# A language-model tower in one kernel: elementwise work of the router and the embedding moved from VectorE to GpSimd, with new instruction orders and later or earlier loads

## The reference

```python
# token stage
x = emb[tokens] * sqrt(128) + positional_encoding
q, k, v = x @ Wq + bq, x @ Wk + bk, x @ Wv + bv
scores = einsum('d,bijd->bij', attn_scale, tanh(q[:, :, None, :] + k[:, None, :, :]))
x = layer_norm(x + softmax(scores) @ v @ Wo + bo)
h = layer_norm(x + relu(x @ W1 + bf1) @ W2 + bf2)
# causal attention with 8 heads of width 128
h = h + attention(layernorm(h))
# mixture of experts, 64 experts, the best 2 per token
t = layernorm(h); hr = _ln(t)
probs = softmax(hr @ Wr @ codebook.T / 0.7)
w = top2(probs) / sum(top2(probs))
hmoe = sum_k w_k * expert_k(hr) + 0.25 * shared(hr)
out = h + t + hmoe + ffn(_ln(hmoe))
```

## Time and profile before

| | us |
|---|---|
| median of 3 runs | 885.13 |
| lowest and highest | 883.92, 888.87 |
| the profiled execution: time | 880.4 |
| the profiled execution: span from the first to the last instruction | 878.6 |

### The profile page before, as it was taken

The page is one execution under the profiler, slowest core; times in us unless marked ns, Lnnn a source line. Parts: engine busy times, 40 slices in busy tenths (PEclk is TensorE's granted clock), DMA queues, the critical chain, the costliest instruction groups (busy, mean ns, idle before and its releaser), DMA issues. The chain is left out here.

```text
span 878.6 us, 22649 instructions
## 1 busy us (share of the span) xinstructions
PE 781.5 (89%) x7286; PEld 603.4 (69%) x7286; DVE 656.6 (75%) x2161; ACT 657.5 (75%) x1502; POOL 323.0 (37%) x397
## 2 busy tenths in 40 slices
PE   1777998988998989989899999898889999999798
PEld 0454675665665766756667666665679999999687
DVE  3999889989999999999999999453523435443675
ACT  2787989989898898988998999675335655655454
POOL 3110322325334343353343432444414545545121
PEclk9999999999999999999999999997989999999799
DMA  7239889889889889989898898894199999994411
GB/s 149 65 83 210 190 188 210 194 189 212 186 196 210 187 198 207 197 189 206 181 211 181 182 209 178 195 208 97 45 321 397 377 395 403 307 362 161 150 30 37
DMA packets 82305, 177.77 MB, mean 202 GB/s; under 512 B 8244, under 2 KB 35339, under 8 KB 82240
## 3 DMA queue, kind: packets, MB, share of 16 engines
q1 hardware_dynamic: 65536, 164.01, 74.8%
q0 software_dynamic: 5760, 7.92, 2.7%
q10 hardware_dynamic: 10944, 5.02, 2.1%
HBM read 65.93 MB, written 113.34 MB: 204 GB/s over the span
## 5 line engine op out<-in xcount | busy, mean ns | idle before, releaser
L890 DVE TENSOR_TENSOR arena<-qT,b_qk 128x2304 f32<-128x2304 f32 x128 | 323.8, 2543 | 1.6 <-DVE v_bias L915 0.3
L616 ACT ACTIVATE arena<-arena 128x2304 f32<-128x2304 f32 x128 | 271.6, 2123 | 35.7 <-DVE arena L890 34.4
L1322 PE MATMUL b_s<-arena,apad 128*32 128x192 f32 x3072 | 159.2, 343 | 27.1 <-ACT p L625 18.5
L771 ACT ACTIVATE act_h<-big,arena 128x128 f32<-128x128 f32 x336 | 95.8, 368 | 74.6 <-PE big L1642 70.2
L1322 PEld LDWEIGHTS b_s<-arena,apad 128*32 128x32 f32 x3072 | 89.9, 113 | 83.9 <-issue 41.5
L542 POOL TENSOR_TENSOR kept<-kept,rs 96x384 f32<-96x384 f32 x64 | 52.6, 823 | 208.2 <-DVE rs L1025 208.0
L590 POOL DMA_INDIRECT eo_dram<-gT,toff x84 | 82.5, 982 | 97.2 <-issue 67.1
L668 ACT ACTIVATE kept<-kept,mx 96x96 f32<-96x96 f32 x256 | 92.3, 365 | 13.3 <-DVE mx L1018 13.3
L1642 PE MATMUL big<-hbT,arena 128*128 128x128 f32 x672 | 91.1, 279 | 2.4 <-DVE hbT L1205 1.4
L1642 PEld LDWEIGHTS big<-hbT,arena 128*128 128x128 f32 x672 | 83.4, 195 | 3.2 <-issue 2.3
L1205 DVE TENSOR_SCALAR hbT<-b_t,cols 128x128 f32<-128x128 f32 x84 | 34.4, 409 | 65.4 <-PE b_t L1635 65.4
(11 more groups left out here) (208 smaller groups left out, 1413.8 us busy)
## 6 DMA issues: line engine op xcount, KB each, us to landing
rows_dram<-act_h SPq DMA_DIRECT2D x32, 3096.0 KB
arena<-in_wpack SPq DMA_DIRECT2D x84, 578.0 KB
prT<-rows_dram ACTq DMA_DIRECT2D x76, 64.5 KB
arena<-eo_dram SPq DMA_DIRECT2D x4, 512.0 KB, 7.2
x_dram<-res SPq DMA_DIRECT2D x16, 96.0 KB
out<-of SPq DMA_DIRECT2D x12, 128.0 KB, 1.8
eo_dram<-gT,toff POOLq DMA_INDIRECT x84
rows_dram<-rows_now,slot_now POOLq DMA_INDIRECT x64
```

The source lines that it names most:

```text
L616: act.activation(v, v, ACT.Tanh).then_inc(s["tanh"], 1)
L771: last = act.activation(act_h[:, i, c * TILE:(c + 1) * TILE], big[i][:, c * TILE:(c + 1) * TILE], ACT.Silu, bias=wslot[:, slot, 2 * DFF + ...
L890: dve.tensor_tensor(ring[c % TRING].rearrange("p (x m n) -> p x m n", m=CQ, n=N), qv.unsqueeze(3).to_broadcast([D, SPLIT * QG, CQ, N]), kv ...
L1322: last = pe.matmul(b_s[32 * a:32 * a + 32, 0:SPLIT * N], apad[:, 31 - line:63 - line], t[:, :, a, m, :], start=(line == 0), stop=(line == ...
```

## The change

- `x_rows` moves from DVE to POOL and becomes two instructions there, a multiplication and an addition with a semaphore (`xm`) between them. It stands in front of `keep_x`.
- `both_hot` and `counted` move from DVE to POOL. The second running count leaves `ranks` on DVE and becomes `cumulated` on POOL. DVE keeps `chosen`, `one_hot` and the rest of `ranks`. Semaphores `topf`, `oh1`, `ohs`, `cum` replace links of DVE's own chain.
- The order of POOL's body changes: `root` for x1 stands ahead of `keep_rows`, not behind it.
- The order of PE's body changes: `pr_turn` 0 ahead of `tn_turn`, `router` ahead of `pr_turn` 1, `score` 2 ahead of `attend1`, `attend2` 1 ahead of `heads_v` 3, `score` 3 ahead of `heads_g` 0, `attend2` 2 ahead of `xs_turn`, `attend2` 3 ahead of `ffn1` 0.
- In ACT's body `v_copy` stands ahead of `tanh` 5.
- SP issues the seven loads of `ld_b` only when the gathers of pair 0 have landed.
- `ROWS_FIRST` is 1: one weight is loaded ahead of the first tile rows.
- The exponential of the gaps is computed on POOL, as a power of a constant, in the expert loop behind the store of tile 12, and the weights by DVE in tiles 21 to 23. ACT's exponential and its two table loads in the tail are gone. Two of the last four `shared_rows` move into the first `mixture`, and PE waits for them only in front of its first `last2`.

```diff
-ROWS_FIRST = 3
+ROWS_FIRST = 1
...
+            sp.wait_ge(s["emb0"], 16 * G)
             load(wvT[:, :], io["tok_WvT"], s["ld_b"])
...
-            sp.wait_ge(s["emb0"], 16 * G)
...
+            def x_rows(p):
+                early = known(p) and p < EARLY
+                if early:
+                    pool.wait_ge(s[f"emb{p}"], 16 * G)
+                else:
+                    gate(pool, s["emb2"], 16 * G * (p - (EARLY - 1)))
...
+                pool.tensor_scalar(xs[:, :, :], pair_of(res, p) if early else emb[:, :, :],
+                                   float(np.float32(D) ** np.float32(0.5)), None, ALU.mult).then_inc(s["xm"], 1)
+                pool.wait_ge(s["xm"], p + 1)
+                pool.tensor_tensor(xs[:, :, :], xs[:, :, :], pe_rows[:, :].unsqueeze(1).to_broadcast([N, G, D]),
+                                   ALU.add).then_inc(s["xs"], 1)
+            def both_hot(p):
+                pool.wait_ge(s["oh1"], p + 1)
+                wait(pool, s["cum"], p)
+                pool.tensor_tensor(ohs[:, :, :], oh[:, :, 0, :], oh[:, :, 1, :], ALU.add).then_inc(s["ohs"], 1)
+            def counted(p):
+                pool.wait_ge(s["ohs"], p + 1)
+                pool.tensor_tensor(cums[:, 1, :], cums[:, 0, :], ohs[:, 0, :], ALU.add).then_inc(s["oh"], 1)
+            def cumulated(p):
+                pool.wait_ge(s["rank_ps"], p + 1)
+                pool.tensor_tensor(cums[:, 0, :], cums[:, 1, :], ohs[:, 1, :], ALU.add).then_inc(s["cum"], 1)
...
                 at(n, 5, scatter_rows, 1)
+                at(n, -1, x_rows)
+                at(n, -1, keep_x)
+                at(n, 1, root, "x1")
+                at(n, 4, both_hot)
+                at(n, 4, counted)
                 at(n, 4, keep_rows)
-                at(n, 1, root, "x1")
+                at(n, 4, cumulated)
                 at(n, 2, normalise, 0)
-                at(n, -1, keep_x)
+                at(n, 3, roots_h1)
...
+            def weigh():
+                pool.wait_ge(s["gaps_t"], 1)
+                pool.tensor_tensor(gap_e[:, :], base_e[:, :], gaps_t[:, :], ALU.pow).then_inc(s["gap_e"], 1)
...
+                at(n, 0, v_copy)
                 at(n, 0, tanh, 5)
-                at(n, 0, v_copy)
...
-            act.preload_act_table(ACT.Exp)
-            act.activation(gap_e[:, :], gaps_t[:, :], ACT.Exp, scale=1.0 / TEMP).then_inc(s["gap_e"], 1)
-            act.preload_act_table(ACT.Silu)
...
+                at(n, 3, pr_turn, 0)
                 at(n, 4, tn_turn)
...
+                at(n, 0, score, 2)
                 at(n, 1, attend1)
-                at(n, 0, score, 2)
```

More of the change, by code:

```diff
@@ L62 @@
 MASKED = 1.0e30
-DVE_LINKS = 14
+DVE_LINKS = 11
 WCOLS = 2 * DFF + FC + D
@@ L879, in qk_evac @@
             def qk_evac(p):
+                if known(p) and p == 0:
+                    dve.wait_ge(s["consts"], 1)
                 dve.wait_ge(s["qk"], p + 1)
@@ L1223, in take_relaid, with weights @@
                     .then_inc(s["gaps_t"], 1)
+            def weights(i):
+                if i == 0:
+                    dve.wait_ge(s["gap_e"], 1)
+                    ch.link(dve.tensor_scalar(gaps_t[:, :], gap_e[:, :], 1.0, None, ALU.add))
+                elif i == 1:
+                    ch.wait()
+                    ch.link(dve.reciprocal(wts[:, :, 0], gaps_t[:, :]))
+                else:
+                    ch.wait()
+                    ch.link(dve.tensor_tensor(wts[:, :, 1], gap_e[:, :], wts[:, :, 0], ALU.mult))
             def add_fbf2(i):
@@ L1250, in _ @@
             eo_copy((last, BLOCK - 1))
-            for j in range(NB - SHARED_LATE, NB):
+            for j in range(NB - SHARED_LATE, NB - 2):
                 shared_rows(j)
-            dve.wait_ge(s["gap_e"], 1)
-            ch.link(dve.tensor_scalar(gaps_t[:, :], gap_e[:, :], 1.0, None, ALU.add))
-            ch.wait()
-            ch.link(dve.reciprocal(wts[:, :, 0], gaps_t[:, :]))
-            ch.wait()
-            ch.link(dve.tensor_tensor(wts[:, :, 1], gap_e[:, :], wts[:, :, 0], ALU.mult))
-            ch.wait()
             def mixture(j):
@@ L1281, in mixture @@
                                           ALU.add))
+                if j == 0:
+                    for i in range(NB - 2, NB):
+                        shared_rows(i)
                 dve.wait_ge(s["frstd"], j + 1)
@@ L1551, in body @@
                 at(n, 0, score, 0)
-                at(n, 3, pr_turn, 0)
                 at(n, 1, p1_turn)
+                at(n, 4, router)
                 at(n, 3, pr_turn, 1)
-                at(n, 4, router)
                 at(n, 0, setup)
@@ L1702, in last2 @@
             def last2(j):
-                if not (known(j) and j == 0):
+                if known(j) and j == 0:
+                    pe.wait_ge(s["ysh"], NB)
+                else:
                     pe.wait_ge(s["of"], j)
```

61 lines of the change are left out of this document (25 added, 36 removed).

## The result

| | before | after |
|---|---|---|
| median, us | 884.52 (4 runs) | 873.14 (4 runs) |
| lowest and highest, us | 883.46, 888.87 | 871.87, 875.17 |
| ratio, with 95% interval | | 0.9873 [0.9835, 0.9911] |
| the profiled execution: time, span | 880.4, 878.6 | 875.17, 873.3 |

The change makes the kernel 1.3% faster; 869 us was predicted, in a range of 857 to 880. The two profiled executions lie only 5.3 us apart, because that of before is quicker than all four runs of its kernel above, and that of after the slowest of its own.

A forecast was written before the change was run, and what follows sets the result against it. A loop of 16.12 us on DVE and 19.06 on PE was taken to set the 35.19 us turn. Terms summed to -16.0: 880.4 to 864.4 us, by the median 869, own range 864 to 875, stated range 857 to 880.

The forecast's parts named there:

- The turn is a loop through p1T and qk; DVE's relief counts 0: Full turns of 35.19 us: DVE and PE alternate; removed DVE work gains 0, PE's order 0.6 a turn, -8.4 us.
- Clock +2: Steady turns: PE's clock dips, swallowed by its waits before, give back about 0.7 us each: +2 us.
- The long turn, -2.0: Turn of 37.18 us: root x1 ahead of keep_rows on POOL ends x1_norm's wait behind a late scatter: -2.0 us.
- The drain, +0.5 for POOL's counts: Behind the last turn, router to scatter: the count chain on POOL is not covered, for two pairs: +0.5 us.
- The first two turns, -0.7: Tower's first two turns: little PE work, so removing x_rows from DVE counts, about 0.35 us each: -0.7 us.
- Between the loops, -2.9 and -2.0 for half clock: Before the expert loop: one weight ahead brings rows sooner, first expert matmul -2.9 us; no half clock after idling, -2.0.
- POOL's power 4.2 us: Expert loop: a 128x24 power takes POOL 4.2 us, but the delay is gone after four stores: 0.
- Tail, -2.3: Behind the expert loop: exponential and table loads gone, first mixture -2.5 us; two moved shared_rows +0.2: -2.3 us.
- (a): Full turns: they shorten by the full 1.05 us and the clock holds, by the median 859 us; chance 0.22.
- (b): Full turns: another loop, ACT the candidate, holds them at 35.2 us, by the median 877.5 us; chance 0.17.
- (c): First row and gathers late for other reasons, turn unchanged; only tail and long turn gain, 881 us; chance 0.10.
- (d): POOL in the turns: x_rows waits for the gather, delaying root x1 and x1_norm; slower, 902 us; chance 0.06.

The follow-up runs named there:

- the two kernels that had one part each: Changed kernel with PE's and ACT's old order, 875.04 us (0.9912); kernel before with only PE's and v_copy's new order, 878.91 us (0.994).
- relief alone: Changed kernel with PE's body and v_copy back in the old order, all other edits kept, POOL's order included: 875.04 us, ratio 0.9912 to the kernel before.

## Why the prediction was right, and where its terms were not

The total was right partly because errors of both signs met: 869 for 873.14, and -9.7 us between the profiles (-11.4 between the medians) for -16.0. The differences below are those of the table's means unless a single profile is named.

- **The turn is a loop through p1T and qk; DVE's relief counts 0** (-8.4 for the order): right and shown, by the two kernels that had one part each. The size was 0.49 a turn instead of 0.6. The count was off too: the third turn is longer (31.0 to 33.1 and more), the fourth is the same (34.17), and the gain starts in the fifth (34.5 to 34.7 for 35.00). Up to the last softmax the tower gave 3.1 us, for 9.3 predicted (8.4 + 0.7 + 2.0 + 0.2 less 2.0; the +0.5 lies behind it). What is missing: the third turn (+2.1 to +3.4, in no term) and the dips.
- **Clock +2**: of the right size, somewhat low. A dip to 0.95 cost 1.1 to 1.4 us, and there are two or three of them: 3.7, 2.2 and 2.3 us in the three profiles. In the kernel before none of the steady turns lost time by a dip. That the tighter turn is the reason isn't shown: relief alone, with turns of 35.19 as before, had three steady dips, and two of them cost 0.86 and 0.85. One turn of after (35.38) is longer at full clock; why is open.
- **The long turn, -2.0**: right, by POOL's order: it is 34.70 for 37.18 (and 38.93 in the second profile of before). But the same wait stands a second time in the kernel before, in the drain, and there the sum hasn't got it.
- **The drain, +0.5 for POOL's counts**: it gave 3.1. From the last softmax to the slots it is 68.3 to 69.4 us for 70.9 and 72.8. The kernel with PE's and ACT's order alone, and POOL's old one, has 71.85, and of the eleven profiles with POOL's new order ten are at 68.3 to 70.0 and one at 71.1. The term that is missing is the wait for root x1 of the last pair, 5.8 us before and 0.84 after. The +0.5 itself is neither shown nor refuted.
- **Start, -0.2**: the first product of the query came at 15.93 us for 15.80. Nothing.
- **The first two turns, -0.7**: about -0.3. The second turn fell from 25.35 to 24.89, and the first maximum came 0.1 later.
- **Between the loops, -2.9 and -2.0 for half clock**: the half clock went, and from the table to the first expert matmul it takes 2.2 us less on the mean, 1.6 in the first pair of profiles (the 2.7 us in time there include an earlier table). The step that failed is that the sum took this start as kept to the end of the loop. Of about 4.9 us nothing is left on the means (-2.2 and +2.7), and with three weights ahead the median was only 0.9 us higher. "Weight 1 goes out at 637.6, some 4 us before use" is right for the first; later weights were late in one of the three profiles.
- **POOL's power 4.2 us**: 4.21 us measured. That nothing is late behind it isn't so in all profiles: a step of 4.7 us four tiles behind it moved with it when it was moved, though it isn't in every profile.
- **Tail, -2.3**: it gave 3.3, as the sum took the median of four loads (3.6 us) for the first, which lands in 2.7 to 2.9 before and after. It also put everything down to the exponential and the moved shared rows at +0.2, where these rows had held DVE about as long. Behind it another 0.7, from a shorter stretch at half clock.

Added up by stretch, the sum was 11.6 us too good in the tower and from the slots to the last expert copy, and 5.3 too bad in the drain and behind the expert loop. That this leaves only 6.3 is luck; the turn, the long turn and the tail are not.

Rivals: (a), 34.1 a turn, is excluded by the 34.70; (b) and (c), which keep 35.2, by the same. (d) didn't come, with POOL waiting up to 2.4 us for the gather.

## What to carry to other kernels

Find the loop that sets a period from waits and starts, and take nothing for work that is removed beside it. When one queue's order is mended for a wait in one turn, look for the same wait elsewhere, in the drain above all, where the turns that would cover it have ended: here the second place gave more than the one in the sum. When a stage starts earlier, don't take the start as kept: look at what its later tiles need, and at the end of the stage in more than one profile. Put a price on dips of the clock that were free before a period was shortened.

## What the runs showed of the hardware

- PE's granted clock fell in turns that are dense: 0.95 over a turn, two or three times in a tower, and not at the same turns in all profiles. In steady turns it cost no time before the change, and 1.1 to 1.4 us each after it. After 3 us without work in front of heads_g it went at half clock.
- A multiply of 96x256 by a constant took 0.86 us on POOL, an add of two tiles of that size 0.72: the operation with fewer operands is the slower.
- SP issued register-addressed loads one per 1.09 us. Weights alone at that rate kept the transfers at 400 GB/s; with a load of 64.5 KB between each two it was 306. ACT's loads of rows landed up to 6 us after their issue, while SP issued weights (three by their issue, eight by their landing); a load of rows has a ninth of a weight's bytes.
